# A mixture-of-experts block: the rows of a block that are not its own get weight zero on VectorE, and the corrected destinations go

## The reference

```python
_, topk_idx = jax.lax.top_k(masked, TOPK)                     # 6 of 32
topk_w = jnp.take_along_axis(scores, topk_idx, axis=1)
g = jnp.einsum('th,ehm->etm', xf, gate_w)                     # m = 176
u = jnp.einsum('th,ehm->etm', xf, up_w)
eo = jnp.einsum('etm,emh->eth', jax.nn.silu(g) * u, down_w)
routed = jnp.einsum('te,eth->th', combine, eo)                # weight of a pair: its score
return (routed + shared).reshape(b, s, h)
```

## Time and profile before

| | us |
|---|---|
| median of 3 runs | 576.58 (573.74 to 577.72) |
| the profiled execution, its own time | 579.25 |
| its span, first to last instruction | 577.5 |
| mean granted clock of TensorE | 0.914 of full speed |

### The profile page before, as it was taken

How to read it: one execution, slowest core, us unless ns; L and a number is a source line. 1 busy time by engine, 2 the same in 40 slices (tenths; PEclk the granted TensorE clock), 3 DMA queues, 4 the chain that set the end, 5 groups by cost and what they waited for, 6 DMA issues and landing times.

```text
span 577.5 us, 9410 instructions
## 1 busy us (share of the span) xinstructions
PE 477.1 (83%) x1970; PEld 320.7 (56%) x1971; DVE 214.9 (37%) x738; ACT 179.1 (31%) x529; POOL 288.2 (50%) x257
## 2 busy tenths in 40 slices
PE   5898987984868999198999989999999998998700
PEld 4455745473525555066666657666767676665400
DVE  2726566466555211022233223223322332332137
ACT  2321323121201222033344335444434443444300
POOL 2304400278777777324555545555645556556422
PEclk9998979888597999688999989999989999999855
DMA  8999510035788964357566555657656566766376
GB/s 284 366 340 370 201 37 1 24 125 177 207 261 282 360 226 155 134 154 136 93 113 106 90 97 97 101 92 127 101 92 105 95 106 95 119 107 99 42 217 237
DMA packets 94400, 89.09 MB, mean 154 GB/s; under 512 B 22601, under 2 KB 88619, under 8 KB 94380
## 3 DMA queue, kind: packets, MB, share of 16 engines
q1 hardware_dynamic: 72492, 58.43, 34.3%
q0 software_dynamic: 19584, 28.33, 26.7%
q10 hardware_dynamic: 2304, 2.10, 1.1%
HBM read 46.88 MB, written 42.99 MB: 156 GB/s over the span
## 4 chain that ended last, share of the span: by engine, by line
DMA 28%; PE 24%; POOL 17%; issue 13%; DVE 6%; ACTq 5%; SPq 4%; ACT 3%; POOLq 1%; DVEq 0%
DMA token_sums<-tok_buf,dest 18%; POOL pair_rows L565 16%; DMA tok_buf<-pair_rows 8%; PE bank L1420 6%; PE bank L1242 4%; ACTq L367 4%; PE bank L1435 3%; PE bank L1228 3%; SPq L367 2%; ACT tok_buf L775 2%; PE bank L1144 1%; DMA XH<-in_L_attn_x 1%; PE bank L1176 1%; PE bank L1413 1%; DVE XH L1137 1%
## 5 line engine op out<-in xcount | busy, mean ns | idle before, releaser
L592 POOL DMA_INDIRECT token_sums<-tok_buf,dest x104 | 162.0, 1558 | 150.6 <-ACT tok_buf L775 70.1
L1420 PE MATMUL bank<-gate_up,tok_buf 128*128 x416 | 147.1, 477 | 10.3 <-DVE tok_buf L1093 9.9
L565 POOL DMA_INDIRECT pair_rows<-XH,rows_i x96 | 94.7, 987 | 61.3 <-DVE rows_i L1018 33.2
L1435 PE MATMUL bank<-down,tok_buf 88*128 x416 | 111.8, 392 | 0.0
L1420 PEld LDWEIGHTS bank<-gate_up,tok_buf 128*128 128x128 f32 x416 | 79.0, 195 | 47.0 <-issue 20.9
L1093 DVE COPY tok_buf<-bank 128x256 f32<-128x256 f32 x104 | 44.2, 425 | 89.1 <-PE bank L1413 87.4
L1435 PEld LDWEIGHTS bank<-down,tok_buf 88*128 88x128 f32 x416 | 72.2, 194 | 8.0 <-issue 0.3
L757 ACT ACTIVATE tok_buf<-bank 128x176 f32<-128x176 f32 x104 | 33.0, 317 | 102.4 <-PE bank L1420 58.8
L775 ACT ACTIVATE tok_buf<-bank,tok_buf 128x256 f32<-128x256 f32 x104 | 49.1, 472 | 32.5 <-PE bank L1435 32.3
L1413 PE MATMUL bank<-ident,tok_buf 128*128 128x128 f32 x208 | 42.2, 286 | 14.8 <-DMA tok_buf<-pair_rows 12.0
L1413 PEld LDWEIGHTS bank<-ident,tok_buf 128*128 128x128 f32 x208 | 28.1, 145 | 47.1 <-issue 25.2
(11 more groups left out here) (150 smaller groups left out, 415.8 us busy)
## 6 DMA issues: line engine op xcount, KB each, us to landing
tok_buf<-pair_rows SPq DMA_DIRECT2D x104, 128.0 KB, 2.9
gate_up<-in_L_ffn_gate_w SPq DMA_DIRECT2D x8, 704.0 KB, 8.5
gate_up<-in_L_ffn_up_w SPq DMA_DIRECT2D x8, 704.0 KB, 8.8
down<-in_L_ffn_down_w SPq DMA_DIRECT2D x2, 2816.0 KB
pair_rows<-sh_rows SPq DMA_DIRECT2D x1, 5120.0 KB, 18.9
gate_up<-token_sums SPq DMA_DIRECT2D x16, 256.0 KB, 5.9
tok_buf<-pair_rows SPq DMA_DIRECT2D x104, 32.0 KB, 2.3
XH<-in_L_attn_x SPq DMA_DIRECT2D x4, 512.0 KB, 9.4
```

Of the source, the lines that this page charges most:

```text
L565: nc.gpsimd.indirect_dma_start(out=pair_rows, out_offset=bass.IndirectOffsetOnAxis(ap=rows_i[:, t, k:k + 1], axis=0), in_=XH[:, t, :], in_ ...
L592: nc.gpsimd.indirect_dma_start(out=token_sums[c % 2], out_offset=bass.IndirectOffsetOnAxis(ap=dest[:, c:c + 1], axis=0), in_=yw[:, c, :], ...
L1420: last = mm(banks[1 + c % 2][:, 0:M2], xT[:, c % 2, k, :], gate_up[:, bass.ds(e * (KC * M2) + k * M2, M2)], start=k == 0, stop=k == KC - 1)
L1435: last = mm(banks[4 + c % 2][:, 0:C], aT[0:KD, c % 2, m, :], down[0:KD, bass.ds(e * C + m * E * C, C)], start=m == 0, stop=m == 1)
```

## The change

`bad_rows` becomes `own_rows` (1 for a block's own row, 0 otherwise), made in two steps. The weight is picked on VectorE in place of ScalarE, as the product of the record's column and the column of `own_rows`; it takes the register load with it. `dest` and its semaphore go: the scatter reads the token numbers from the record itself, and the rows that are not the block's own are added with weight zero. The tile of zeros from which the segments' heads are cleared has T as its token number, by an iota on POOL, so that rows which no pair ever filled are still dropped by the bounds check.

```diff
--- before.py
+++ after.py
@@ -95,8 +95,7 @@
         sT = sb("sT", [P, len(SC), W])
         sh_rows = sb("sh_rows", [P, 2, C])
         zeros = sh_rows[:, :, :].rearrange("p s c -> p (s c)")[:, 0:XW]
-        bad_rows = sb("bad_rows", [P, P])[:, :]
-        dest = sb("dest", [P, 4], i32)
+        own_rows = sb("own_rows", [P, P])[:, :]
         rows_i = sb("rows_i", [P, NT, TOPK], i32)
         ident = sb("ident", [P, P])
         iota_e = sb("iota_e", [P, E])
@@ -197,7 +196,6 @@
         x1_back = sem("x1_back")
         sel_ready, recs_ready, dispatched = (sem(n) for n in ("chosen_ready", "rows_ready", "rows_dispatched"))
         zeros_ready, sums_clear, heads_clear = sem("zeros_ready"), sem("token_sums_clear"), sem("segment_heads_clear")
-        dest_ready = sem("destinations_ready")
         sh_stored = [sem(f"shared_rows_stored{s}") for s in range(2)]
         mapf_ready = sem("map_columns_ready")
         gb_ready, gb_stored, gb_back = sem("gate_rows_ready"), sem("gate_rows_stored"), sem("gate_rows_back")
@@ -505,7 +503,8 @@
                 ins.then_inc(pool_own, 1)
                 pool.wait_ge(pool_own, done[0])
 
-            nc.gpsimd.memset(sh_rows[:, :, :], 0.0).then_inc(zeros_ready, 1)
+            link(nc.gpsimd.memset(sh_rows[:, :, :], 0.0))
+            nc.gpsimd.iota(zeros[:, C + E:C + E + 1].bitcast(i32), [[0, 1]], base=T, channel_multiplier=0).then_inc(zeros_ready, 1)
 
             link(nc.gpsimd.memset(ident[:, :], 0.0))
             nc.gpsimd.affine_select(out=ident[:, :], in_=ident[:, :], compare_op=ALU.not_equal, fill=1.0,
@@ -586,11 +585,10 @@
 
 
                 pool.wait_ge(y_scaled, n + 1)
-                pool.wait_ge(dest_ready, n + 1)
                 wait(pool, scattered[(c - 2) % R], 16 * turns)
                 pool.sem_inc(pool_passed, 1)
                 nc.gpsimd.indirect_dma_start(
-                    out=token_sums[c % 2], out_offset=bass.IndirectOffsetOnAxis(ap=dest[:, c:c + 1], axis=0),
+                    out=token_sums[c % 2], out_offset=bass.IndirectOffsetOnAxis(ap=rec[:, c, E:E + 1].bitcast(i32), axis=0),
                     in_=yw[:, c, :], in_offset=None, bounds_check=T - 1, oob_is_err=False,
                     compute_op=ALU.add).then_inc(scattered[c], 16)
 
@@ -763,11 +761,6 @@
                 nc.scalar.activation(aT[0:KD, c % 2, :, :], banks[3][0:KD, 0:2 * P].rearrange("p (m n) -> p m n", m=2),
                                      ACT.Copy).then_inc(aT_copied, 1)
 
-            def pick_weight(c, turn, e):
-
-                act_e.wait_ge(rec_loaded[c], 16 * turn + 16)
-                nc.scalar.activation(pair_weight[:, c:c + 1], rec[:, c, bass.ds(e, 1)], ACT.Copy).then_inc(weight_ready, 1)
-
             def weigh(c, n):
 
                 act_e.wait_ge(y_done, n + 1)
@@ -778,10 +771,7 @@
             await_read(act_e, ("map",))
             silu(0, 0)
 
-            A = mybir.EngineType.Activation
-
             def step(turn, last):
-                experts = load_values(act_e, A, 0, turn, 0)
                 for c in range(R):
                     n = R * turn + c
                     if not last or c + 1 < R:
@@ -789,7 +779,6 @@
                     copy_act(c, n)
                     if not first(n):
                         weigh((c - 1) % R, n - 1)
-                    pick_weight(c, turn, experts[c])
                     if last and c == R - 1:
                         weigh(c, n)
 
@@ -1075,10 +1064,9 @@
             link(V.memset(map_i, 0))
             link(V.tensor_copy(map_i[0:1, 2 * MAP_W:2 * MAP_W + 1], mapf[0:1, 2:3]))
             ps = await_result(dve, ("map",))
-            link(V.tensor_scalar(bad_rows, ps[:, 2 * P:3 * P], iota_p[:, 0:1], None, ALU.is_gt))
-            link(V.scalar_tensor_tensor(out=bad_rows, in0=ps[:, 3 * P:4 * P], scalar=iota_p[:, 0:1], in1=bad_rows,
-                                        op0=ALU.is_le, op1=ALU.max))
-            link(V.tensor_scalar(bad_rows, bad_rows, float(T), None, ALU.mult))
+            link(V.tensor_scalar(own_rows, ps[:, 2 * P:3 * P], iota_p[:, 0:1], None, ALU.is_le))
+            link(V.scalar_tensor_tensor(out=own_rows, in0=ps[:, 3 * P:4 * P], scalar=iota_p[:, 0:1], in1=own_rows,
+                                        op0=ALU.is_gt, op1=ALU.mult))
             V.tensor_copy(map_i[0:1, 0:2 * MAP_W].rearrange("p (a n) -> p a n", a=2)[:, :, 1:P + 1],
                           ps[0:1, 0:2 * P].rearrange("p (a n) -> p a n", a=2)).then_inc(free(("map",)), 1)
             await_read(dve, ("map",))
@@ -1098,27 +1086,26 @@
                     dve.wait_ge(act_turned, n - 1)
                 V.tensor_tensor(act[:, c % 2, :], act_g[:, c % 2, :], banks[1 + c % 2][:, M:M2], ALU.mult).then_inc(act_done, 1)
 
-            def bound_tokens(c, turn, n):
+            def pick_weight(c, turn, n, e):
                 dve.wait_ge(rec_loaded[c], 16 * turn + 16)
-                V.tensor_tensor(dest[:, c:c + 1], rec[:, c, E:E + 1].bitcast(i32), bad_rows[:, bass.ds(n, 1)],
-                                ALU.max).then_inc(dest_ready, 1)
+                V.tensor_tensor(pair_weight[:, c:c + 1], rec[:, c, bass.ds(e, 1)], own_rows[:, bass.ds(n, 1)],
+                                ALU.mult).then_inc(weight_ready, 1)
 
             for c in range(2):
                 copy_x(c, c)
             multiply(0, 0)
 
+            D = mybir.EngineType.DVE
+
             def step(turn, last):
-
+                experts = load_values(dve, D, 0, turn, 0)
                 for c in range(R):
                     n = R * turn + c
-                    if not first(n):
-                        bound_tokens((c - 1) % R, turn - (c == 0), n - 1)
                     if not last or c + 2 < R:
                         copy_x(c, n + 2)
                     if not last or c + 1 < R:
                         multiply(c + 1, n + 1)
-                    if last and c == R - 1:
-                        bound_tokens(c, turn, n)
+                    pick_weight(c, turn, n, experts[c])
 
             blocks(dve, step)
 
```

## The result

The changed kernel takes 581.50 us (median of 11 runs, 574.47 to 584.99), the kernel before 573.74 beside it (11 runs, 570.78 to 577.72). The ratio is 1.0096, with a 95% interval of 1.0066 to 1.0125. So it is slower, by 1.0% in the one and 1.4% in the other.

What follows compares the result with a forecast made beforehand. Slot 3's loop through DMAs was taken to bound the blocks; -7.0 us for shorter turns and +1.0 for added rows made -6.0, so 576.6 became 570.6 us, range 559 to 583.

Steps and rivals of the forecast that it cites:

- the bound before: Blocks: slot 3's loop of scatter, record load, pick, register load and weigh bounds the old kernel at 10.65 us a turn.
- the load on VectorE: Head of each turn: the register load moved to VectorE begins at word 1 + 4 * turn and takes 2.15 us.
- the time from pick to gate and up: Turn's start: from the pick's start on VectorE through load and copy to TensorE's gate and up, 3.21 us.
- the new two-turn loop: Blocks: record, load, copy, gate and up, steps, down and scatter span two turns, so a late landing counts half.
- the picks as such and POOL's wait: ScalarE's pick time and POOL's wait on destinations: removing them is worth nothing, taken as zero.
- Rival A: VectorE's load costs little: 564.6 us with a load of 1.67 us, 557 with 0.59; chance 0.2.
- the price of the new loop: Blocks: TensorE stalls 0.53 us a turn, turns take 10.50, mean 11.08 against 11.36, so -7.0 us over 25 turns.
- a sign of being wrong: The forecast called itself wrong if TensorE's stall at the head of a turn is over 0.8 us.
- rival B: Slower: the register load stands before copy_x and takes 2.75 us, mean turn 11.68, 585.6 us; chance 0.18.
- the base: Old mean turn of 11.36 us from the profiled execution of 579.25 us; the change was put to the median, 576.6.
- C: No change: the scatters' tables take over as bound, landings of 4.5 us, mean turn 11.30, 576 us; chance 0.2.
- the added rows: Scatters: up to 1,024 more rows added with weight zero cost +1.0 us, ends 0 and +8.7.

Runs made afterwards that it cites:

- e4: Kernel before, with ScalarE's register load beginning at word 4 * turn instead of 1 + 4 * turn: 561.24 us, 0.9805 of the kernel before.
- e2: Changed kernel with pick and register load back on ScalarE, weight zero made there, no corrected destinations: 571.28 us, 0.9981 of the kernel before.
- e8: e2 with ScalarE's and SyncE's register loads both beginning at a word divisible by four: 554.89 us, 0.9659 of the kernel before.
- e3: Changed kernel with VectorE's register load beginning at word 4 * turn instead of 1 + 4 * turn: 563.74 us, 0.9839 of the kernel before.
- e12: The changed kernel timed and profiled once more, nothing altered: 580.18 us, 1.0135 of the kernel before.
- e1: Kernel before with pick and register load moved to VectorE, corrected destinations kept, so no added rows: 580.12 us, 1.0122 of the kernel before.
- e9: e3 with a copy of about 1.35 us that nothing reads behind the load, after the record's wait: 583.96 us, 1.0205 of the kernel before.
- e10: e3 with load and pick moved ahead of the wait for slot 3's record, plus the 1.35 us unused copy: 562.52 us, 0.9826 of the kernel before.
- e7: e4 with SyncE's register load also beginning at a word divisible by four: 558.61 us, 0.9730 of the kernel before.

## Why the prediction was wrong

**Right:** the bound before (slot 3's loop, which e4 shortened by ACT's load alone, for 11 us); that the load on VectorE begins where it takes long, and its length (1.98 for 2.15); the time from pick to gate and up (409.25 to 412.52: 3.27 for 3.21); the new two-turn loop; that the picks as such and POOL's wait are worth nothing while the long load is there (e2; e8 has 0.7% for the waits without it). Rival A's price was too good: with a load of 0.59 it had 557, 19.5 us under the kernel before, and e3, with 0.65, is 9 us under.

**The step that failed is the price of the new loop.** "...+3.98 landing; +0.16 issue; +1.95; +0.12: the pick of slot 3 starts 9.12 after the start" gave turns of 10.50. In the chain above the loop of two turns is 21.95, so 10.97 a turn in this pair. Of the 0.95 us over the forecast 21.00, the record's landing is 0.49 (2.44, not 1.95), the scatter's 0.10 (4.08, not 3.98), the hand-over from the pick 0.06, and the rest, 0.3, TensorE's steps and POOL's start. The 1.95 came from a turn of the kernel before, while the prediction itself had the median 2.3 of all record loads beside it. In that turn the loop had been short because this landing was. The stall that follows is 10.97 - 9.96 = 1.01 us a turn in this pair. Over all turns gate and up's wait for `copy_x` is 19.9 us, or 0.80 for each of 25 turns (22.5 and 0.90 in e12), where the forecast had 0.53 and named over 0.8 as a sign of being wrong. So rival B is what happened, by its mechanism (the load stands before `copy_x`), though not by its cause, a load of 2.75 us, nor by its mean turn of 11.68.

A stretch in which none of the three traces has a fall of the granted clock shows it too. From the seventh scatter of slot 3 to the 23rd, the mean of 16 turns is 10.80 in the changed kernel (337.63 to 510.48) and 10.90 in e12 (339.38 to 513.80), against 10.82 in e2 (334.96 to 508.02), which keeps the load on ACT. The forecast had 10.92 for the old loop and 10.64 for the new one without the long turns. The old one, by e2, came out near that; the 0.28 us a turn that the new one was to save did not come at all.

**A second term was mis-sized: the base.** The prediction set 11.08 us a turn against 11.36 and took the difference for the gain. The 11.08 was near (11.04 in the profile of 574.47 us, 11.15 in that of 578.42, 11.52 in e1's of 585.29). The 11.36 was that of one execution, 5.5 us above the median of later runs, with three stretches of granted clock under 0.9 between 260 and 440 us, in the turns of 13.07, 13.16 and 12.35; e2, with the time of the kernel before (its profile: 572.95), has no such stretch before 540 us, and 10.99 a turn. The forecast took the difference from the profiled execution and put it to the median, and that cancels only if the profiled execution is typical in its turns. It was not. An estimate, if the 5.5 us lie in the blocks: they are 0.22 a turn, so 11.14 for a median execution, and the forecast's own 11.08 would then have given a gain of 1.5 us and not of 7.

**A third was left out: the first turn.** From the start of SyncE's first register load to the first scatter it is 254.9 - 239.6 = 15.3 us before, as in e2 (256.1 - 240.7 = 15.4), but 257.6 - 241.0 = 16.6 in the changed kernel: the load stands on the chain there too, ahead of the third block's copy. That is 1.3 us.

**The old stalls against the new.** In the kernel before TensorE also waited; 254 to 530 us (who waited for whom, us in total, times, longest):

```profile
DVE tok_buf L1099 <- ACT tok_buf L757: 41.2, 24, 2.3
...
PE bank L1420 <- DVE tok_buf L1093: 9.5, 13, 2.1
PE bank L1428 <- DVE tok_buf L1099: 7.2, 13, 0.8
```

And in the changed kernel, where `multiply` no longer waits for ACT:

```profile
PE bank L1407 <- DVE tok_buf L1081: 19.9, 16, 2.1
```

9.5 + 7.2 = 16.7 us in 26 pieces of 0.64 became 19.9 in 16 pieces of 1.24. The sum is little more even though the profile of before is a slow execution, but each piece is twice as long. Whether long pieces cost more than their length is less clear. In e1 (windows of 4 us: length, busy PE, PEld, DVE, ACT, POOL, clock, DMA share, GB/s):

```profile
296.00:300.00 4.00, 4.00 (x19) 2.78 (x17) 1.30 (x6) 1.75 (x5) 1.91 (x2) 1.00 0.75 106
300.00:304.00 4.00, 1.73 (x10) 1.16 (x9) 0.92 (x4) 1.17 (x3) 2.63 (x2) 1.00 0.51 79
304.00:308.00 4.00, 4.00 (x12) 2.94 (x13) 1.19 (x7) 0.70 (x2) 1.55 (x1) 0.60 0.78 134
308.00:312.00 4.00, 4.00 (x19) 2.87 (x19) 0.80 (x4) 1.64 (x4) 1.56 (x1) 0.97 0.28 48
```

TensorE is busy for 1.73 of 4 us from 300 to 304, and then the granted clock is 0.60 from 304 to 308. e1's profile has four such places between 270 and 480 us, the changed kernel's one (2.14 us for gate and up at 301.37 in place of 1.35, behind 2.11 us of idle), e2's none. That a long stall brings the clock down is what the order in these rows suggests. But it isn't a rule by these traces: in e12 gate and up starts behind 2.48, 2.29 and 2.05 us of idle at 269.14, 303.19 and 371.99 without a fall, and behind 1.66 at 325.94 with one (2.33 us for gate and up); and the kernel before has falls too, behind 2.09 and 1.79 us of idle (265.52 and 337.06) and behind only 0.85 (426.34). No run tried it alone, and e12 shows that it isn't the whole spread, so what the falls add to the loss stays open.

**Of the rivals:** C is partly in the new loop, since the scatter of slot 1 (419.13) lands just when slot 3's (424.37) would start anyway. That the added rows cost 1.0 us is not borne out: e2 allows -2.5 to +0.3 for them and the saved waits together.

## What to carry to other kernels

Before an instruction that holds a queue for 2 us is moved to another engine, write down what stands ahead of it and behind it there: behind a wait for data and ahead of the copy that feeds TensorE 35 us of work (26 times 1.35) cost 21 us; one place earlier, where the engine idles, it costs about a quarter of that (e9 and e10). Price a new loop with the medians of its transfers, not with those of the one turn in which the old loop was shortest; and take the ground that a forecast is measured from out of several executions. And look at where a table begins that several engines read into registers: one word less was worth more here than the whole change (e4: 2%, e7: 2.7%).

## What the runs showed of the hardware

- Loading eight consecutive words of SBUF into registers takes 0.52 to 0.65 us when it begins at a word divisible by four, and 1.67 to 2.00 when it begins one word after (medians), on SyncE (0.53 against 1.67 to 1.82), ScalarE (0.57 against 1.93) and VectorE (0.65 against 1.98). TensorE has both in every run: 0.59 in the turns and some 2.75 ahead of the first one. Other starts and other lengths weren't tried, so whether eight bytes or sixteen decide is open. The Trainium skill, "Runtime: NRT & Kernel Launch", section "Instruction fetch mechanics", has about 200 ns for a register even in bulk, for loads that the page describes as coming from HBM; that agrees with the loads that begin one word after (1.67 / 8 = 0.21), and not with the others (0.53 / 8 = 0.07).
- Rows that the bounds check drops moved no bytes: the scatters' queue moved 28.33 MB with the corrected destinations (e1) and 28.64 MB without (e2), in 19,584 packets both times.
- Executions of the same kernel differ by 1.8% (574.47 to 584.99 for the changed kernel), more than the change is worth.
